# One PSUM bank of the attention scores changes its ring: two for the maxima, three for the exponentials

## The chip, the cores and the metric

The kernel runs on one core of a Trainium2 chip. The metric is the device time of one execution in microseconds. The kernel before takes 1253.35 us, the median of three runs (1252.35 to 1255.59).

## What is computed

Four sequences of 512 tokens with 512 channels go through two attention layers and a mixture of experts. Cut to what matters:

```python
# layer 1, x: (4, 512, 512), 16 heads of 32
xn = rms_norm(x, g_norm) * (1 + scale) + shift          # scale, shift from cond
q, k, v = split(xn @ W_qkv); q, k = rms_norm(q, g_q), rms_norm(k, g_k)
o = softmax(q @ k.T / sqrt(32)) @ v
y = o + o @ W_out
# layer 2: latent projections, rotary parts, causal attention
h = y + softmax(causal(q2 @ k2.T / sqrt(32))) @ v2 @ o_w
# 1 shared and 7 routed experts, the best two of them for each token
out = x + h + shared(rms_norm(h)) + sum(w_e * expert_e(rms_norm(h)))
```

Each softmax is over 512 keys, and its row maximum is subtracted before the exponential.

## The kernel before, in words

The attention of both layers is one loop over 512 steps. There are 8 batches (`k`): 0 to 3 are the four sequences in layer 1, 4 to 7 the same in layer 2, which is causal. A batch has 64 steps: 8 pairs of heads, in each pair 8 steps, which alternate between the two heads (`side`) and go through the four blocks of 128 tokens (`t`). `head_step` turns a step's number M into these.

For each step a block of scores is computed twice. `scores(M)` (matmul L939) writes scores with queries on the partitions, 128x512, and VectorE takes their row maximum (L1722 in layer 1; L1725 in layer 2, where a block is only (t+1)*128 wide and a second small instruction reads the accumulator). After each pair the maxima are transposed (`turn_max`, L948), ScalarE copies them (L1140, `max_rows`), and a DMA (L565) puts them as one more row under the pair's stacked operands (`stack`). `scores_t(M)` (L960, in layer 2 with a second small matmul for the mask, L963) then writes the transposed scores, keys on the partitions, with the maximum already subtracted by that row. ScalarE takes their exponential into `probs` (L1298), and `pv(M)` (L976; two rows of the trace for one product) multiplies them with the values. So each step's PSUM traffic goes through two rings of banks: `sq`, which is filled by L939 and cleared by the maximum, and `sk`, which is filled by L960 and cleared by the exponential.

The eight PSUM banks are dealt out by hand: 0 and 1 are the ring of all other work, `sq` has 2, 3 and 6, `sk` has 4 and 5, and 7 gathers the products with the values. A ring's item m lies in bank `banks[m % n]`, and `wait_free` before filling waits for the clearing of item m - n:

```python
def wait_free(self, eng, m):
    m = self.item(m)
    if m >= self.n:
        eng.wait_ge(self.free[m % self.n], m // self.n)
```

The order of every engine's work is written out. TensorE's loop does for step M: the scores of step M + 16 (`LEAD`), now and then `turn_max`, the transposed scores of step M, every fourth step the four products of steps M - 5 to M - 2 (`LAG`, `GROUP`), and then what the table `beside_heads` puts beside this step:

```python
for M in range(NSTEPS + LAG):
    if M + LEAD < NSTEPS:
        scores(M + LEAD)
    if M < NSTEPS:
        if max_turn(M) is not None:
            turn_max(max_turn(M))
        scores_t(M)
    if (M - LAG) % GROUP == GROUP - 1 and M > LAG:
        for n in range(GROUP):
            pv(M - LAG - GROUP + 1 + n)
```

Before the loop the scores of the first 16 steps are computed alone; this is called the lead below. Beside the steps go the projections (L793 to L795), transposes (L802), the output product and the splitting of fp32 values into a high and a low part. VectorE does the maximum of step M + 16 and then its own share of the table: scaling of transposed values out of PSUM (L1573, L1575), low halves (L1563), reciprocals and division, and the chains of norms (L1553 to L1559). ScalarE does the exponential of step M and then copies, squares and high halves. GpSimd makes low halves and squares in SBUF. A step of the table stands at the same step on each engine, with a step's delay for some. No scheduler reorders anything; each engine takes its list in program order.

After the loop the tiles of the experts use the same banks: transposed rows in 4 and 5 (`XB`), gate and up in 2 and 3 (`GB`), transposed hidden values in 6 (`HB`), the down product in 7. Their first uses wait for the last readers of those banks in the loop (`tile_turn`, `gate_up`, `turn_h`).

Of the kernel before, what the change touches and what calls it, by code (L numbers as in the profile page):

```python
# [42 lines left out]
NSTEPS = NB * STEPS_H  # L43
# [258 lines left out]
def build(nc, x_d, cond_d, wemb_d, bemb_d, gnorm_d, wqkv_d, gq_d, gk_d, wout_d, ln1_d, ln2_d, kvd_d,  # L302
# [11 lines left out]
    with ExitStack() as ctx:  # L314
        sem = lambda name: ctx.enter_context(nc.semaphore(name))
# [149 lines left out]
        r_ld, x1_ld, acc_ok, acc_st, x2_st = sem("second_x_loaded"), sem("residual_loaded"), sem("acc_ready"), sem("acc_stored"), sem("x2_rows_stored")  # L465
        lg_ok = sem("logits_ready")
        ring = Ring("ring", sem, (0, 1), RING_NO)
        sq = Ring("scores", sem, (2, 3, 6))
        sk = Ring("scoresT", sem, (4, 5))
        o = Ring("pv", sem, (7,))  # L470

        es_ld, es_hi, es_lo = (sem(f"shared_{x}") for x in ("loaded", "hi", "lo"))
# [313 lines left out]
        def _(pe):  # L786
# [226 lines left out]
            def tile_turn(i):  # L1013
                if i in ROUTED:
                    pe.wait_ge(xg_got[i % 2], 16 * (ROUTED.index(i) // 2 + 1))
                else:
                    pe.wait_ge(xg_ld[i % 2], 16 * (i // 2 + 1))
                if i >= 2:
                    pe.wait_ge(x_lo, i - 1)
                else:  # L1020
                    sk.wait_read(pe, NSTEPS - 2 + i)
                for c in range(NC):
                    last = nc.tensor.transpose(psum[:, XB[i % 2], c * P:(c + 1) * P], xg[:, i % 2, c * P:(c + 1) * P],  # L1023
                                               ident[:, :])
                last.then_inc(t_mm, 1)
# [34 lines left out]
            def turn_h(i):  # L1060
                q = i % 2
                pe.wait_ge(h_v, i + 1)
                if i >= 2:
                    pe.wait_ge(h_lo, i - 1)
                elif i == 0:
                    sq.wait_read(pe, NSTEPS - 3)
                for n in range(NI):
                    last = nc.tensor.transpose(psum[:, HB, (q * NI + n) * P:(q * NI + n + 1) * P],  # L1068
                                               hv[:, q, n * P:(n + 1) * P], ident[:, :])
                last.then_inc(h_mm, 1)  # L1070
# [23 lines left out]
            def table_product(n):  # L1094
# [5 lines left out]
                last.then_inc(g_mm_r, 1)  # L1100

            tile_turn(0)
            tile_turn(1)
            beside(("back", LAST, NPR - 1))
            gate_up(0, 0)
# [4 lines left out]
            for s in range(NTILES):  # L1110
                if s + 1 < NTILES:
                    gate_up(s + 1, 0)
                turn_h(s)
                if s + 2 < NTILES:
                    tile_turn(s + 2)
                if s == X2_SLOT:
                    beside(("x2", LAST, 0))
                    beside(("x2", LAST, 1))
                if s == ROUTER_SLOT:
                    beside(("router", LAST, 0))  # L1120
                for n in TABLE_MID.get(s, ()):
                    table_product(n)
                if s + 1 < NTILES:
                    gate_up(s + 1, 1)
                if s == COUNT_SLOT:
                    count_product()
                for n in TABLE_LATE.get(s, ()):
                    table_product(n)
                down(s)
                if s == X2_SLOT:  # L1130
                    beside(("x2", LAST, 2))
                    beside(("x2", LAST, 3))
                if s == ROUTER_SLOT:
                    beside(("router", LAST, 1))
# [897 lines left out]
```

## Time and profile before

| what | value |
|---|---|
| median of 3 runs | 1253.35 us (1252.35 to 1255.59) |
| profiled execution, own time | 1256.78 us |
| its span | 1255.0 us |
| TensorE busy in the span | 1145.3 us (91%) |
| VectorE / ScalarE / GpSimd busy | 728.1 / 572.9 / 333.9 us |
| mean granted clock of TensorE | 0.96 |
| lead, attention loop, rest | 77 to 89, 89 to 912, 912 to 1255 us |

The profile is of one execution. An engine's busy time counts its instructions, and for TensorE the matmuls; PEld are the weight loads that go ahead of them. In a row of a wait or a group, what stands behind the arrow ended the engine's idle time. The chain of work that ended last is 73% TensorE.

### The profile page before, as it was taken

Reading aid. Unit: us, or ns where it says so; the run is one execution under the profiler, and the core shown is the slowest. Engines: PE = TensorE matmul, PEld = TensorE weight load, DVE = VectorE, ACT = ScalarE, POOL = GpSimd, SP = SyncE. Lnnn points to the kernel's source line nnn. Section 1 sums busy time; section 2 is a strip of 40 time slices with the busy share of each in tenths; the row PEclk is TensorE's granted clock in tenths of the full one; section 3 lists DMA queues with packets and bytes.
Section 4 is the critical chain, followed back from the end, with each engine's and each line's share of the span. In section 5 each row is a group of like instructions: output and inputs, shape, how many; then the busy total and the mean of one; then the engine's idle time right before and its main releaser. Section 6 shows DMA issues by size and latency. Waiting matters only on the chain.

```text
span 1255.0 us, 18112 instructions
## 1 busy us (share of the span) xinstructions
PE 1145.3 (91%) x5687; PEld 798.4 (64%) x5687; DVE 728.1 (58%) x1714; ACT 572.9 (46%) x1248; POOL 333.9 (27%) x275
## 2 busy tenths in 40 slices
PE   5989989999999899999989899989989999999960
PEld 5755545665666456557657667755657888888850
DVE  6465486468545865656646766574545764444433
ACT  3324365445544565555455555544456743222310
POOL 0413133201320231002022202200235644555530
PEclk9969999999999899999989999998999999999985
DMA  7153344336322742553584473486567735656569
GB/s 262 34 168 118 98 145 130 90 98 202 120 64 89 228 131 64 184 168 105 175 229 140 144 247 95 144 250 162 145 215 249 250 126 106 109 111 116 106 147 328
DMA packets 105609, 191.10 MB, mean 152 GB/s; under 512 B 24140, under 2 KB 34796, under 8 KB 103980
## 3 DMA queue, kind: packets, MB, share of 16 engines
q1 hardware_dynamic: 96700, 169.61, 43.7%
q0 software_dynamic: 8512, 19.93, 8.9%
q8 instruction: 49, 0.80, 0.3%
q10 hardware_dynamic: 304, 0.40, 0.1%
q14 instruction: 44, 0.36, 0.1%
HBM read 118.98 MB, written 65.53 MB: 147 GB/s over the span
## 4 chain that ended last, share of the span: by engine, by line
PE 73%; DMA 8%; DVE 7%; SPq 4%; issue 3%; ACT 3%; POOL 1%; DVEq 0%; ACTq 0%; POOLq 0%
PE psum L976 12%; PE psum L793 9%; PE psum L794 8%; PE psum L795 8%; PE psum L939 6%; PE psum L960 6%; PE psum L1054 4%; PE psum L1056 4%; PE psum L1055 4%; PE psum L802 3%; PE psum L1081 2%; SPq L554 2%; PE psum L1083 2%; PE psum L1082 2%; PE psum L1023 2%
## 5 line engine op out<-in xcount | busy, mean ns | idle before, releaser
L1298 ACT ACTIVATE probs<-psum 128x512 f32<-128x512 f32 (+3 forms) x512 | 257.4, 517 | 217.2 <-PE psum L963 108.9
L1722 DVE TENSOR_REDUCE nmax<-psum 128x1 f32<-128x512 f32 x256 | 171.3, 686 | 124.2 <-PE psum L939 119.4
L939 PE MATMUL psum<-stack 96*128 96x512 f32 (+3 forms) x512 | 211.0, 417 | 10.1 <-DVE nmax L1725 6.7
L976 PE MATMUL psum<-probs,vals 128*33 128x512 f32 (+3 forms) x1024 | 212.3, 537 | 0.0
L960 PE MATMUL psum<-stack 97*128 97x512 f32 (+3 forms) x512 | 199.7, 391 | 11.8 <-ACT probs L1298 6.2
L1725 DVE CUSTOM_DVE_ANT_0 psum<-psum,causal 128x128 f32<-128x128 f32 (+3 forms) x256 | 123.8, 503 | 74.6 <-PE psum L939 73.6
L939 PEld LDWEIGHTS psum<-stack 96*128 96x128 f32 x512 | 100.5, 196 | 83.2 <-issue 58.4
L960 PEld LDWEIGHTS psum<-stack 97*128 97x128 f32 x512 | 99.7, 195 | 38.8 <-ACT probs L1298 16.7
L1433 POOL TENSOR_TENSOR o_lo<-o_chunk,o_hi 128x512 fp32r<-128x512 f32 x31 | 42.0, 1354 | 276.4 <-ACT o_hi L1140 276.4
L976 PEld LDWEIGHTS psum<-probs,vals 128*33 128x33 f32 x1024 | 50.0, 112 | 101.5 <-issue 76.4
L793 PE MATMUL psum<-w_hi,xh 128*128 128x512 f32 (+1 forms) x256 | 96.8, 378 | 5.2 <-POOL xl L1401 3.6
L794 PE MATMUL psum<-w_hi,xl 128*128 128x512 f32 (+1 forms) x256 | 94.9, 371 | 0.0
L795 PE MATMUL psum<-w_lo,xh 128*128 128x512 f32 (+1 forms) x256 | 94.6, 370 | 0.0
L1501 POOL DMA_INDIRECT acc_s<-tile_y,row_of_slot x38 | 60.5, 1591 | 82.4 <-DVE tile_y L1802 74.0
L1140 ACT ACTIVATE qk<-psum 128x512 f32<-128x512 f32 (+1 forms) x64 | 31.5, 493 | 101.6 <-PE psum L795 101.4
L1339 ACT ACTIVATE tile_h_hi<-psum 128x256 fp32r<-128x256 f32 x54 | 20.8, 385 | 99.2 <-PE psum L1068 98.8
L793 PEld LDWEIGHTS psum<-w_hi,xh 128*128 128x128 f32 x256 | 49.3, 193 | 22.6 <-issue 6.7
L1054 PE MATMUL psum<-routed_hi,tile_x_hi 128*128 x152 | 62.6, 412 | 0.0
L963 PE MATMUL psum<-mask,identr 128*128 128x128 f32 x256 | 61.4, 240 | 0.0
L1420 POOL TENSOR_TENSOR vs<-qk 128x512 f32<-128x512 f32 x32 | 33.6, 1051 | 103.3 <-ACT qk L1140 103.3
L1401 POOL TENSOR_TENSOR split<-vs,split 128x512 fp32r<-128x512 f32 x16 | 21.2, 1328 | 146.9 <-ACT split L1140 146.9
L1056 PE MATMUL psum<-routed_lo,tile_x_hi 128*128 x152 | 59.6, 392 | 0.0
(245 smaller groups left out, 2283.1 us busy)
## 6 DMA issues: line engine op xcount, KB each, us to landing
stack<-split_s SPq DMA_DIRECT2D x378, 128.0 KB, 3.3
split_s<-split SPq DMA_DIRECT2D x64, 512.0 KB, 3.9
inverse_sums<-inverse_s SPq DMA_DIRECT2D x31, 256.0 KB
xt<-in_x_dram SPq DMA_DIRECT2D x4, 1024.0 KB, 5.3
x_s<-yt SPq DMA_DIRECT2D x4, 1024.0 KB, 5.6
xt<-x_s SPq DMA_DIRECT2D x4, 1024.0 KB, 5.3
res<-x_s SPq DMA_DIRECT2D x4, 1024.0 KB, 10.3
yt<-in_x_dram SPq DMA_DIRECT2D x4, 1024.0 KB, 6.0
```

The lines of the kernel that those rows point to most:

```text
L793: nc.tensor.matmul(out, ah, bh, start=(i == 0), stop=False)
L794: nc.tensor.matmul(out, al, bh, start=False, stop=False)
L795: last = nc.tensor.matmul(out, ah, bl, start=False, stop=(i == n - 1))
L939: sq.filled(nc.tensor.matmul(psum[:, sq.bank(M), 0:n], st[:, 0, t * P:(t + 1) * P], st[:, 1, 0:n], start=True, stop=True), M)
L960: last = nc.tensor.matmul(psum[:, bank, lo:S], st[:, 1, t * P:(t + 1) * P], st[:, 0, lo:S], start=True, stop=not masked)
L963: last = nc.tensor.matmul(psum[:, bank, lo:lo + P], identr[:, :], mask[:, :], start=False, stop=True)
L976: nc.tensor.matmul(psum[at_:at_ + VW, o.bank(p), lo:S], vals[k % 2][:, t, head_of(q, side), :], probs[:, M % NX, lo:S], start=(t == 0), st ...
L1054: nc.tensor.matmul(out, xth[:, q, c, :], weight(i, 0, c), start=(c == 0), stop=False)
L1056: last = nc.tensor.matmul(out, xth[:, q, c, :], weight(i, 1, c), start=False, stop=(c == NC - 1))
L1298: sk.cleared(nc.scalar.activation(probs[:, M % NX, lo:S], psum[:, sk.bank(M), lo:S], ACT.Exp, scale=SCALE), M)
L1722: sq.cleared(V.tensor_reduce(out, psum[:, sq.bank(M), :], AX.X, ALU.max, negate=True), M)
L1725: sq.cleared(V.tensor_tensor_reduce(out=x, in0=x, in1=causal[:, (NT - 1 - t) * P:], scale=-1.0, scalar=-NEG, op0=ALU.add, op1=ALU.min, acc ...
```

## The change

The third bank of the scores for the maxima, bank 6, becomes the third bank of the transposed scores. The waits after the loop follow: `tile_turn` for tiles 0 and 1 waits for the exponentials of the last three steps, and `turn_h` for the last one, since bank 6 is now read by ScalarE. Instructions and their order are the same on every engine. Below the second hunk all line numbers grow by one.

```diff
-        sq = Ring("scores", sem, (2, 3, 6))
-        sk = Ring("scoresT", sem, (4, 5))
+        sq = Ring("scores", sem, (2, 3))
+        sk = Ring("scoresT", sem, (4, 5, 6))
...
                 if i >= 2:
                     pe.wait_ge(x_lo, i - 1)
                 else:
-                    sk.wait_read(pe, NSTEPS - 2 + i)
+                    for m in range(NSTEPS - 3, NSTEPS):
+                        sk.wait_read(pe, m)
...
                 elif i == 0:
-                    sq.wait_read(pe, NSTEPS - 3)
+                    sk.wait_read(pe, NSTEPS - 1)
```

## Rows read from the trace of the kernel before

**Rows 1.** The page, busy us of each engine (share of the span) xinstructions.
```profile
PE 1145.3 (91%) x5687; PEld 798.4 (64%) x5687; DVE 728.1 (58%) x1714; ACT 572.9 (46%) x1248; POOL 333.9 (27%) x275
```
**Rows 2.** Stretches: length, then PE, PEld, DVE, ACT, POOL busy; clock, DMA share, GB/s.
```profile
77.00:89.00 12.00, 10.72 (x20) 5.54 (x21) 10.55 (x18) 1.36 (x3) 2.93 (x5) 0.50 0.89 259
89.00:447.00 358.00, 344.16 (x1489) 207.08 (x1488) 226.82 (x404) 179.86 (x361) 84.15 (x68) 0.97 0.41 125
447.00:912.00 465.00, 436.69 (x2423) 296.70 (x2421) 281.39 (x878) 243.59 (x600) 73.02 (x72) 0.97 0.55 160
722.20:725.60 3.40, 3.40 (x12) 1.16 (x9) 1.77 (x6) 0.21 (x1) 0.00 (x0) 0.50 0.41 138
174.60:180.00 5.40, 5.40 (x23) 3.16 (x24) 4.03 (x6) 3.76 (x9) 3.78 (x3) 1.00 0.45 151
```
**Rows 3.** Waits of PEld, the weight loads: us in total, times, longest us.
```profile
PEld psum L960 <- ACT probs L1298: 16.7, 34, 1.8
...
PEld psum L939 <- DVE nmax L1725: 9.9, 13, 2.1
...
PEld psum L939 <- DVE nmax L1722: 4.4, 11, 1.5
```
**Rows 4.** Waits of PE, the matmuls: us in total, times, longest us.
```profile
PE psum L960 <- ACT probs L1298: 6.2, 17, 1.4
```
**Rows 5.** Groups by form: busy us, mean ns of one, then idle before, releasers.
```profile
L1298 ACT ACTIVATE probs<-psum 128x512 f32<-128x512 f32 x320 | 184.8, 596 | 127.5 <-PE psum L960 105.8 <-PE psum L963 21.0
L1722 DVE TENSOR_REDUCE nmax<-psum 128x1 f32<-128x512 f32 x256 | 171.3, 686 | 124.2 <-PE psum L939 119.4
```
**Rows 6.** Waits of DVE: us in total, times, longest us.
```profile
DVE nmax L1722 <- PE psum L939: 119.4, 76, 6.1
DVE psum L1725 <- PE psum L939: 73.6, 73, 3.7
```
**Rows 7.** Timeline at 174 us: start, us, engine, line, operation, [idle before].
```profile
173.41 0.64 ACT L1140 ACTIVATE wout_hi<-wout_raw 128x512 fp32r<-128x512 f32 x1
173.93 0.61 ACT L1298 ACTIVATE probs<-psum 128x512 f32<-128x512 f32 x1
...
174.59 0.19 PEld L960 LDWEIGHTS psum<-stack 97*128 97x128 f32 x1 [1.80 <-ACT probs L1298]
```
**Rows 8.** Timeline at 323 us, steps 143 to 145 of the scores.
```profile
323.03 0.80 DVE L1575 TENSOR_SCALAR vs<-psum,modall 128x512 f32<-128x512 f32 x1
...
323.32 0.19 PEld L939 LDWEIGHTS psum<-stack 96*128 96x128 f32 x1
...
323.98 0.69 DVE L1722 TENSOR_REDUCE nmax<-psum 128x1 f32<-128x512 f32 x1
...
324.11 1.91 PE L976 MATMUL psum<-probs,vals 128*33 128x512 f32 x8
...
325.53 0.69 DVE L1722 TENSOR_REDUCE nmax<-psum 128x1 f32<-128x512 f32 x1
```
**Rows 9.** Timeline of the lead and of the loop's first steps.
```profile
78.73 9.65 DVE L1722 TENSOR_REDUCE nmax<-psum 128x1 f32<-128x512 f32 x16
...
87.87 0.29 PEld L939 LDWEIGHTS psum<-stack 96*128 96x128 f32 x1 [0.94 <-DMA stack<-split_s]
...
88.70 0.69 DVE L1722 TENSOR_REDUCE nmax<-psum 128x1 f32<-128x512 f32 x1 [0.32 <-PE psum L939]
...
89.32 0.33 PEld L939 LDWEIGHTS psum<-stack 96*128 96x128 f32 x1
```
**Rows 10.** Timeline at 905 us, the last scores of the loop.
```profile
905.87 0.14 DVE L1725 DVE_READ_ACCUMULATOR2_ANT nmax<- 128x1 f32 x1
905.87 0.19 PEld L939 LDWEIGHTS psum<-stack 96*128 96x128 f32 x1
```
**Rows 11.** Timeline at 721 us, a wait for a maximum.
```profile
721.36 0.44 PE L939 MATMUL psum<-stack 96*128 96x384 f32 x1 [0.98 <-DVE nmax L1725]
```

## The prediction

> **What bounds the kernel now.** I start with the page's busy times [rows 1]: TensorE is busy 1145.3 of 1255.0 us, VectorE 728.1. The table by stretches [rows 2] splits that. The attention loop runs from 89 to 912 us; in its first half (batches in the order of the first layer) TensorE is busy 344.16 of 358.00 us, in the second (the causal layer) 436.69 of 465.00. So TensorE, which takes everything in program order, is the bound in both, and whatever makes it wait is paid in full unless it was about to wait anyway.
>
> The change touches two of its waits. Before writing scores of step M (L939) TensorE waits until VectorE's maximum has left that bank; before the transposed scores (L960) until ScalarE's exponential has. Today the first wait looks three steps back, the second two. The wait tables show what each costs: the weight loads of L960 wait 16.7 us for ScalarE in 34 places, those of L939 9.9 and 4.4 us for VectorE in 13 and 11 [rows 3]. The matmul rows, which hide a wait shorter than the matmul before it, show 6.2 us in 17 places for L960 [rows 4]. So the scarce side on record is the one that gets the bank. What the tables do not show is how much the third bank now saves on the other side; for that I go to the durations and the timeline.
>
> A maximum takes 686 ns and an exponential 596 ns on 512 columns [rows 5]. VectorE, though the idler engine, carries the bulky extras between maxima, and it waits for TensorE 119.4 and 73.6 us in 76 and 73 places [rows 6]: mostly it is early, and in bursts late.
>
> **The change, part by part.**
>
> *No instruction is added or moved.* Each engine keeps its rows; only which step's release a matmul waits for differs. At the tail `tile_turn` takes three waits where it had one, and `turn_h` waits for the last exponential instead of a maximum. The products with the values before them in TensorE's program already waited for those exponentials. Both cost nothing; that cover is gone only if the tail moved ahead of the last products.
>
> *Gain: the exponentials get three banks.* A typical place is 174.59 us [rows 7]: ScalarE has a weight copy before exponential 43, which ends at 173.93 + 0.61; TensorE's load for transposed scores 45 stands idle 1.80 us for it. With three banks it would need exponential 42, long done. The products behind do need 43, but only the last of the four does, and eight rows of products (two per product) take 1.91 us [rows 8], so three of them cover about 1.4 us. Going along all 512 transposed scores, I find about 50 loads that start within 75 ns of the end of the exponential two steps before, most at the steps in which the four products follow; their excess over the normal pitch of 0.235 us sums to 11.2 us. The tables bound it from below by 6.2 and from above by 16.7 us. I take 11.2 less 2.8 for those places in which VectorE's wait then stands in the same spot, **-8.4 us**.
>
> *Loss, in the lead.* From 78.73 us VectorE does 16 maxima in 9.65 us, 0.603 us each, and paces TensorE [rows 9]. At the clock of that stretch (0.50 of full, 1.2 GHz, [rows 2]) a load that was let go at 87.87 us is followed by its maximum at 88.70, 0.83 us later. With two banks two maxima need 0.69 + 0.05 + 0.83 = 1.57 us (0.05 is the shortest time seen from a release to a load), 0.785 each. So 14 x 0.18 = 2.6 us more. The load at 87.87 ends a wait of 0.94 us for a transfer that does not depend on this; it swallows as much. **+1.7 us**.
>
> *Loss, beside the lead.* With two banks a load of L939 must start 0.05 us after the maximum two steps before ends. The first place where it would not is early: maximum 16 ends at 88.70 + 0.69 = 89.39, load 18 stands at 89.32, 0.12 us short [rows 9]. The typical large one is at 323 us [rows 8]: VectorE alternates maxima with value scalings (0.80 us, L1575), 1.5 us a step, while TensorE puts two scores back to back ahead of four products. Load 145 starts at 323.32; maximum 143 runs from 323.98 to 324.67. Short by 1.40 us, and the 1.91 us of products behind it move as a block. Maximum 145 began at 325.53 because VectorE was late, not TensorE; hence it stays, and the shift ends in TensorE's time alone.
>
> I compare each of the 496 loads after the lead with that release: 112 are short, by 71 us together. That sum is wrong as a price, since a shift made by the first serves the next. In each stretch I carry the shift along: it becomes the larger of itself and the next shortfall, is reduced by any wait for VectorE that stands in the row today, and is booked when VectorE again waits for TensorE. The first stretch is that of 89.32 us, the last that of 905.87 us, where maximum 509 is read until 906.01 and the load is 0.19 short [rows 10]. There are 41 stretches with 25.2 us: by batches 6.4, 4.0, 2.9, 2.9 in the first layer, 1.5, 2.7, 1.2, 3.5 in the causal one, where today's waits of L939 [rows 3] already pay for much of it. **+25.2 us**.
>
> *A page's rule.* In the rows at 323 us rotation through banks alone does not overlap the read: maximum 143 starts 0.66 us after load 145 already stands. The Trainium skill, page "Perfetto Trace Analysis", section "Optimizing Tensor Performance", says that independent groups of matmuls should rotate through different banks so that one's evacuation overlaps the next group's work, and names no depth. Read so, two banks would do, and the loss beside the lead would be nought; the row speaks against it, and it comes back among the rivals.
>
> *Clock.* The loop runs at 0.97 of full clock on average, that is mostly at 2.4 GHz with a few stretches at 1.2. One of these lasts from 722.20 to 725.60 us [rows 2], right behind a wait for a maximum of 0.98 us [rows 11], and TensorE is busy through all of it. Half its 3.40 us, 1.7 us, is what such a stretch costs. New waits of over 1 us may bring one more or none: bounds 0 and 11 x 1.7 us, since 11 of my stretches are longer than 1 us. The idle 1.80 us at 174.59 brought none: behind it the clock is 1.00 [rows 2, 7]. So I take one, **+1.7 us**.
>
> Sum: -8.4 + 1.7 + 25.2 + 1.7 = **+20.2 us** on the profiled execution, whose own time is 1256.8 us for a span of 1255.0. That one lies 3.4 us above the median of the three runs, 1253.35. Against the median I forecast **1273.5 us**. A measurement of this kernel can tell about 0.3%, 3.8 us, from no change.
>
> **The rivals.**
>
> *Every wait cools the clock.* The clock falls behind most of the 11 long waits: 11 x 1.7 = 18.7 instead of 1.7 us, +37 us, **1290 us**. For: 722.20 lies right behind such waits. Against: the idle time at 174.59 us, which no fall follows. The Trainium skill, page "TensorE: Matmul & The Clock Gate", section "A second HAM failure mode: psum-queue depth-cycling", describes this for a kernel that cycles through banks, with small idle times between groups and a clock that swings. 15%.
>
> *VectorE's lateness spreads.* My carrying rule assumes that a late maximum holds only TensorE. If the extras behind it (scalings, low halves) come late too and TensorE waits for them, each stretch counts with its largest shortfall and nothing is swallowed: 39 + 1.7 + 1.7 - 8.4 = +34 us, **1287 us**. For: ScalarE and GpSimd follow VectorE's scalings. Against: today's waits of that kind are few. 12%.
>
> *Two banks are enough, and the third pays where it goes* (the other side, and the page's rule). TensorE is late itself when it reaches the scores: the lead of 16 steps keeps the loads behind, the first shift of a batch leaves VectorE a head start that lasts, and nothing but the lead's 1.7 us is lost, against a gain of 8.4 us or, by [rows 3], at most 16.7: -6.7 to -15.0 us, **1238 to 1247 us**. It decides if the load at 323 us comes 1.4 us later by itself. For: VectorE waits 193 us for TensorE in all [rows 6]. Against: a head start is lost whenever it waits, since its extras are tied to steps. 6%.
>
> *They cancel.* Losses half of mine, gain full: 12.6 + 1.7 - 11.2 = +3.1 us, **1256.5 us**. 6%.
>
> **How the numbers follow.** Forecast 61%, rivals 15, 12, 6 and 6%. The time is that of the forecast. The range reaches down to the forecast's terms at their kind ends (-16.7 + 1.7 + 25.2 + 0 = +10.2 us, 1263.5) less a little for stretches that I price too high, 1260, and up past both slower rivals, 1293. Out of it lie the last two rivals and some of the tail. Faster by over 0.3%: 0.06; within: 0.06; slower: 0.88.
>
> **What would show it.** Right: the loads of L939 wait for maxima some 30 to 45 us instead of 14.3, the loads of L960 for exponentials nearly nothing, with a few us turned up at the products' loads; the lead's 16 maxima take about 12 us instead of 9.65; at the place of 323 us a load stands idle some 1.4 us; the time after the loop is unchanged. Of the added time, two thirds lie in the first layer. Wrong: the attention loop is no longer than 823 us (my carrying rule fails), or L960 still waits for ScalarE (then the exponentials' lateness is more than one step deep), or the granted clock of the loop falls well below 0.97 (then the first rival).

## The result, and the profile after

The changed kernel takes 1268.82 us, the median of four runs (1263.02 to 1276.72), against 1254.47 us for the kernel before beside it: a ratio of 1.0113, 95% interval 1.0082 to 1.0145, so 14 us or 1.1% slower. Run again on another occasion (below), the ratio was 1.0121 (1.0094 to 1.0148). The forecast was 1273.5 us, 20 above the kernel before, in a range of 1260 to 1293.

The profiled execution of the changed kernel took 1266.78 us, its span is 1265.0. TensorE is busy 1149.0 us where it was 1145.3. Its weight loads wait, by the table of waits (us in total, times, longest us; of before see [rows 3]; lines above 1018 are one higher now):

```profile
PEld psum L939 <- DVE nmax L1723: 35.0, 48, 3.4
PEld psum L939 <- DVE nmax L1726: 20.3, 28, 2.7
...
PEld psum L976 <- ACT probs L1299: 3.7, 6, 0.7
```

The loads of the scores now wait 55.3 us for maxima where it was 14.3. The loads of the transposed scores no longer appear with ScalarE at all: the 16.7 us are gone. They did not turn up at the products' loads, as the forecast expected: those (L976) wait 3.7 us for exponentials, where it was 16.3. Where the time lies shows best when both traces are cut at the same four places: the first score, the first transposed score, the first transposed score of layer 2, and the last product with the values. First the kernel before, then the changed one, columns as in [rows 2]:

```profile
77.10:88.00 10.90, 9.71 (x18) 4.69 (x18) 9.88 (x17) 1.26 (x3) 2.93 (x5) 0.50 0.89 255
88.00:550.20 462.20, 444.95 (x1957) 265.93 (x1957) 290.85 (x549) 239.29 (x489) 99.30 (x83) 0.98 0.43 129
550.20:929.40 379.20, 353.03 (x2054) 248.19 (x2053) 225.19 (x754) 195.37 (x498) 66.62 (x62) 0.96 0.57 167
929.40:1255.00 325.60, 280.81 (x1422) 231.74 (x1422) 161.44 (x318) 112.97 (x218) 147.31 (x99) 0.94 0.65 167
```
```profile
75.60:89.30 13.70, 11.18 (x18) 4.67 (x19) 10.62 (x17) 1.23 (x3) 2.92 (x5) 0.50 0.83 243
89.30:557.90 468.60, 448.22 (x1957) 264.58 (x1958) 291.63 (x551) 239.81 (x489) 98.61 (x83) 0.98 0.42 126
557.90:939.50 381.60, 354.04 (x2054) 250.30 (x2052) 226.63 (x753) 195.49 (x497) 66.56 (x62) 0.96 0.57 165
939.50:1265.00 325.50, 281.03 (x1424) 231.85 (x1422) 161.64 (x319) 113.08 (x218) 147.28 (x99) 0.94 0.65 168
```

The lead is 2.8 us longer, layer 1 6.4, layer 2 2.4, the rest 0.1 shorter. The first score happened to start 1.5 us earlier, which makes the 10.0 us between the spans. The granted clock of each piece is the same to the two digits shown, but in layer 2 the changed kernel's trace has 34 us at half clock and that of before 27.

The typical place of [rows 8], the turn from batch 1 to batch 2, is there as forecast: load 145 has to wait for maximum 143. Timeline of the changed kernel, steps 143 to 145:

```profile
330.72 0.19 PEld L939 LDWEIGHTS psum<-stack 96*128 96x128 f32 x1 [0.23 <-issue]
...
331.47 0.69 DVE L1723 TENSOR_REDUCE nmax<-psum 128x1 f32<-128x512 f32 x1
...
332.22 0.19 PEld L939 LDWEIGHTS psum<-stack 96*128 96x128 f32 x1 [1.18 <-DVE nmax L1723]
...
332.89 1.91 PE L976 MATMUL psum<-probs,vals 128*33 128x512 f32 x8
```

Load 145 is the one at 332.22. It waits for maximum 143 to end at 332.16 and starts 0.06 us later; the products are behind it.

### The profile page after: what moved, and what is told of

Same layout as the page of the kernel before. It is cut to its first block, busy times and chain, and to the rows that moved or that the text cites. A ratio compares the mean times of both kernels' runs of the same rounds, so it can differ in the third digit from the quotient of the medians.

```text
span 1265.0 us, 18114 instructions
## 1 busy us (share of the span) xinstructions
PE 1149.0 (91%) x5687; PEld 797.1 (63%) x5687; DVE 731.3 (58%) x1714; ACT 573.7 (45%) x1248; POOL 333.1 (26%) x275
## 4 chain that ended last, share of the span: by engine, by line
PE 74%; DVE 9%; DMA 7%; SPq 3%; issue 3%; ACT 3%; POOL 0%; DVEq 0%; ACTq 0%; POOLq 0%
PE psum L976 13%; PE psum L793 9%; PE psum L795 8%; PE psum L794 8%; PE psum L939 8%; PE psum L960 6%; PE psum L1055 4%; PE psum L1057 4%; PE psum L1056 4%; PE psum L802 3%; PE psum L1082 2%; PE psum L1084 2%; PE psum L1083 2%; PE psum L1024 2%; DVE nmax L1723 2%
## 5 line engine op out<-in xcount | busy, mean ns | idle before, releaser
L939 PE MATMUL psum<-stack 96*128 96x512 f32 (+3 forms) x512 | 216.3, 426 | 32.1 <-DVE nmax L1726 15.3
L976 PE MATMUL psum<-probs,vals 128*33 128x512 f32 (+3 forms) x1024 | 214.5, 542 | 0.0
L960 PE MATMUL psum<-stack 97*128 97x512 f32 (+3 forms) x512 | 195.3, 382 | 3.3 <-DMA stack<-max_rows 3.2
L939 PEld LDWEIGHTS psum<-stack 96*128 96x128 f32 x512 | 100.2, 196 | 121.9 <-issue 57.7
L976 PEld LDWEIGHTS psum<-probs,vals 128*33 128x33 f32 x1024 | 50.4, 113 | 104.3 <-issue 92.0
L960 PEld LDWEIGHTS psum<-stack 97*128 97x128 f32 x512 | 100.2, 196 | 16.8 <-DMA stack<-max_rows 4.2
L793 PE MATMUL psum<-w_hi,xh 128*128 128x512 f32 (+1 forms) x256 | 95.6, 374 | 4.0 <-POOL xl L1402 2.3
L793 PEld LDWEIGHTS psum<-w_hi,xh 128*128 128x128 f32 x256 | 48.6, 190 | 21.3 <-issue 6.7
```

Source lines behind the costliest of these rows:

```text
L793: nc.tensor.matmul(out, ah, bh, start=(i == 0), stop=False)
L939: sq.filled(nc.tensor.matmul(psum[:, sq.bank(M), 0:n], st[:, 0, t * P:(t + 1) * P], st[:, 1, 0:n], start=True, stop=True), M)
L960: last = nc.tensor.matmul(psum[:, bank, lo:S], st[:, 1, t * P:(t + 1) * P], st[:, 0, lo:S], start=True, stop=not masked)
L976: nc.tensor.matmul(psum[at_:at_ + VW, o.bank(p), lo:S], vals[k % 2][:, t, head_of(q, side), :], probs[:, M % NX, lo:S], start=(t == 0), st ...
```

## The experiments

All ratios are to the kernel before, run in turn with them on the same chip. Four sets ran together: `two_two`, `layer2_exp`, `layer1_exp` and `lead_max`; `by_need` and `by_no_need`; `changed_again`, `two_two_again`, `need_idle` and `by_need_again`; and the last two.

### What is the exponentials' third bank worth?

`two_two` leaves bank 6 unused in the loop:

```diff
         sq = Ring("scores", sem, (2, 3))
-        sk = Ring("scoresT", sem, (4, 5, 6))
+        sk = Ring("scoresT", sem, (4, 5))
```

> Two banks for the maxima, two for the exponentials, bank 6 idle: the loss of the change without its gain. Theory (the third bank was worth 8 us to the exponentials, and that much of the loss was paid back): about 8 us above the changed kernel, 22 above the one before, and the loads of L939 wait for maxima about as long as in the changed kernel. Rival (once the loads of L939 wait for VectorE, ScalarE is never late, so the exponentials' third bank is worth nothing): equal to the changed kernel within 2 us, and the loads of L960 wait for exponentials under 4 us.

Measured: 1266.73 us, ratio 1.0091 (1.0069 to 1.0113). That is not above the changed kernel's 1.0113. My theory asked for about 1.018, so it falls, and the rival holds in its first half. In its second, under 4 us of waits for exponentials, it does not: the loads of L960 still waited 7.2 us. Since the two had not stood beside each other, I ran both once more:

> The changed kernel unaltered, to stand beside the next one on one chip. Both theories: 11 to 14 us above the kernel before.

> Bank 6 idle, on the same chip as the changed kernel. Theory as it stands now (ScalarE is late in the same stretches as VectorE, so a wait for a maximum covers what the exponentials' third bank would save): within 2 us of the changed kernel, at most 2 above. Rival (the third bank of the exponentials is worth the 8 us that I put on it): 8 above it.

Measured: 1268.13 us, 1.0121 (1.0094 to 1.0148), and 1268.25 us, 1.0122 (1.0097 to 1.0147). In the time as a whole the third bank of the exponentials is worth nothing that can be measured; by the two intervals up to some 4 us either way would not have shown. The waits of `two_two`'s loads:

```profile
PEld psum L939 <- DVE nmax L1723: 34.7, 48, 2.6
PEld psum L939 <- DVE nmax L1726: 18.2, 26, 3.0
PEld psum L976 <- ACT probs L1299: 16.2, 52, 0.4
PEld psum L960 <- ACT probs L1299: 7.2, 17, 0.8
```

Of the 16.7 us for exponentials before, more than half is gone though the exponentials got no bank: the likely reading is that TensorE, held back by the new waits for maxima, comes later to the exponentials' banks. What became of the other 7.2 can be seen where my forecast took its example [rows 7]. The changed kernel, loads of scores 61, 62 and 63, and what VectorE does meanwhile:

```profile
175.48 0.19 PEld L939 LDWEIGHTS psum<-stack 96*128 96x128 f32 x1 [1.07 <-DVE nmax L1723]
...
177.99 0.19 PEld L939 LDWEIGHTS psum<-stack 96*128 96x128 f32 x1 [0.84 <-issue]
...
178.47 1.19 DVE L1555 TENSOR_SCALAR rst<-sst 128x4 int32<-128x4 int32 x1
179.69 1.19 DVE L1556 TENSOR_SCALAR rst<-rst 128x4 int32<-128x4 int32 x1
180.91 0.69 DVE L1723 TENSOR_REDUCE nmax<-psum 128x1 f32<-128x512 f32 x1
...
181.66 0.19 PEld L939 LDWEIGHTS psum<-stack 96*128 96x128 f32 x1 [3.37 <-DVE nmax L1723]
```

and the second run of `two_two`:

```profile
176.54 0.19 PEld L939 LDWEIGHTS psum<-stack 96*128 96x128 f32 x1 [0.92 <-DVE nmax L1723]
...
177.54 0.19 PEld L960 LDWEIGHTS psum<-stack 97*128 97x128 f32 x1 [0.81 <-ACT probs L1299]
...
179.81 0.19 PEld L939 LDWEIGHTS psum<-stack 96*128 96x128 f32 x1 [0.84 <-issue]
...
182.73 0.19 PEld L939 LDWEIGHTS psum<-stack 96*128 96x128 f32 x1 [2.63 <-DVE nmax L1723]
```

With two banks the load of transposed scores 45 waits 0.81 us for an exponential; with three it does not, and load 62 comes 2.51 instead of 3.27 us after load 61. Then load 63 waits 3.37 instead of 2.63 us, and from load 61 to load 63 it is 6.18 us in the one and 6.19 in the other. TensorE reaches the next wait for VectorE earlier and waits there.

How much is left in sum can be read from the waits of all matmuls added up, whatever they wait for: 68.7 us before, 76.6 and 75.7 in the two profiles of `two_two`, 74.7 in both of the changed kernel. So the exponentials' third bank saves 1 to 2 us of TensorE's waits, not 8.

That leaves the clock, and there the two kernels differ. The mean granted clock is 0.963 in the 74 executions of the kernel before that ran beside the experiments, 0.957 in the 10 of the changed kernel and 0.961 in the 11 of `two_two`. What is missing to a full clock, (1 - clock) times the span, is 45.9, 54.8 and 49.5 us on average, with standard errors of 0.4, 1.3 and 1.3. So a small gain of the third bank may be eaten by a lower clock. Single profiles do not settle it. Layers 1 and 2 in `changed_again` and then in `two_two`:

```profile
89.90:559.30 469.40, 448.27 (x1957) 265.11 (x1957) 291.12 (x549) 239.91 (x489) 98.41 (x83) 0.98 0.41 126
559.30:937.20 377.90, 350.88 (x2054) 248.24 (x2053) 225.99 (x754) 195.84 (x498) 66.44 (x62) 0.96 0.57 167
```
```profile
90.10:560.20 470.10, 449.58 (x1958) 265.58 (x1958) 291.10 (x551) 240.00 (x489) 98.36 (x83) 0.98 0.42 125
560.20:943.20 383.00, 353.74 (x2054) 248.91 (x2053) 226.91 (x754) 196.34 (x498) 66.79 (x63) 0.96 0.57 166
```

In layer 2, at a clock of 0.96 in both, `changed_again` is 5.1 us shorter; but the two other profiles of the same kernels have it the other way round, 381.60 us at 0.96 and 378.50 at 0.98. Why the clock is lower with three banks for the exponentials stays open.

### Where does the loss sit: which layer, and the lead?

For these, bank 6 changes hands during the loop. Each of banks 2 to 6 gets one pair of semaphores, a table is dealt out in TensorE's program order, and a matmul takes the bank of its set that was used longest ago. Instructions and their order stay. The matmuls after the loop wait for the last readers of both sets. Only the rule that says for which scores m bank 6 belongs to the maxima differs; it stands for RULE in this cut.

```diff
-        sq = Ring("scores", sem, (2, 3))
-        sk = Ring("scoresT", sem, (4, 5, 6))
+        full, free = ({b: sem(f"scores_{x}{b}") for b in (2, 3, 4, 5, 6)} for x in ("full", "free"))
+        of = deal(RULE)
+        sq, sk = Dealt(of["sq"], full, free), Dealt(of["sk"], full, free)
...
+    for M in range(-LEAD, NSTEPS):
+        S_ = M + LEAD
+        mine = third_to_maxima(S_)
+        if S_ < NSTEPS:
+            take("sq", (2, 3, 6) if mine else (2, 3))
+        if M >= 0:
+            take("sk", (4, 5) if mine else (4, 5, 6))
```

`layer2_exp`, with the rule `m < 16 + 4 * STEPS_H`:

> Bank 6 goes to the maxima in the lead and in layer 1, to the exponentials in layer 2. Theory (loss where VectorE alternates bulky work with full-width maxima, which is layer 1): 0 to 4 us above the kernel before, and layer 1 as long as before. Rival (the loss belongs to the ring, in whatever layer): half of the measured 14 us, so 7 above.

Measured: 1255.4 us, 1.0004 (0.9987 to 1.0021). Level with the kernel before, as the theory had it; the rival's 7 us are outside. In its profile layer 1 takes 460.10 us (462.20 before). In layer 2 the loads of scores wait 18.7 us for maxima, 8.8 more than before, and those of the transposed scores 8.4 us less for exponentials, and the time is level.

`layer1_exp`, with `m >= 16 + 4 * STEPS_H`:

> The mirror image: bank 6 goes to the exponentials in the lead and in layer 1, to the maxima in layer 2. Theory: 9 to 12 us above the kernel before. Rival (loss even over the layers): 7 above.

Measured: 1265.74 us, 1.0096 (1.0065 to 1.0127), 12 us by the ratio and 10 between the medians: the lead and layer 1 carry the loss. Its profile has a lead of 13.70 us and 470.60 us for layer 1:

```profile
76.20:89.90 13.70, 11.17 (x18) 4.66 (x18) 10.59 (x17) 1.25 (x3) 2.93 (x5) 0.50 0.84 243
89.90:560.50 470.60, 449.66 (x1957) 265.39 (x1957) 291.05 (x549) 240.14 (x489) 98.47 (x83) 0.98 0.42 125
```

`lead_max`, with `m < LEAD`:

> The changed kernel, but the 16 scores of the lead take three banks in turn. Theory (each two maxima of the lead need 1.57 instead of 1.21 us): the lead is 2.5 to 3 us shorter than in the changed kernel and the rest the same, so 2 to 3 us below it. Rival (the transfer of the stack ends last anyway): no shorter than the changed kernel.

Measured: 1265.29 us, 1.0090 (1.0063 to 1.0117). The runs don't tell it from `two_two` beside it. The profile does: the lead is back at 10.90 us, with 16 maxima in one go again, and layer 1 stays as long as in the changed kernel.

```profile
75.60:86.50 10.90, 9.77 (x18) 4.76 (x19) 9.89 (x17) 1.24 (x3) 2.94 (x5) 0.50 0.84 254
86.50:555.20 468.70, 447.57 (x1957) 264.63 (x1957) 291.17 (x551) 240.01 (x489) 98.73 (x83) 0.98 0.42 127
```

So the lead costs 2.8 us; that the whole program is shorter by as much is consistent with the runs and not shown by them.

### Is it the places where VectorE is late?

The 20 stretches are those in which a load of L939 in the trace of before stands less than 0.05 us behind the end of the maximum two steps back, with the two scores ahead of it, and with stretches merged that have at most three scores between them; they begin with scores 0 to 33 and end with 458 to 511. They hold 256 of the 512 scores, so that the mirror image shares bank 6 exactly as evenly.

> Bank 6 belongs to the maxima for 256 of the 512 scores, in 20 stretches: those in which the trace of the kernel before shows a maximum two steps back that is late for a load of L939 (the lead among them). In the other 256 it belongs to the exponentials. Theory (the loss of the change sits where VectorE is late, nowhere else): as fast as the kernel before, within 2 us, or up to 3 us faster if the exponentials gain in the other half. Rival (the maxima need their third bank anywhere, in proportion to the steps): 6 us above the kernel before.

Measured: 1251.36 us, 0.9985 (0.9972 to 0.9998).

> The mirror image: bank 6 belongs to the exponentials in those 20 stretches and to the maxima in the other 256 scores. Theory: as slow as the changed kernel, 11 to 14 us above the kernel before, with the loads of L939 waiting for maxima over 45 us. Rival (in proportion to the steps): 6 us above.

Measured: 1267.45 us, 1.0116 (1.0093 to 1.0140). With bank 6 the same half of the time in maxima's hands, one is level with the kernel before or a hair faster and the other as slow as the changed one. The rival, 6 us for each, is out. So the place decides; part of the difference may come by way of the clock, whose mean is 0.965 in `by_need` and 0.958 in `by_no_need`. The waits of `by_need` and then of `by_no_need` (their lines are shifted: L991 is the scores, L1012 the transposed ones, L1028 the products):

```profile
PEld psum L1012 <- ACT probs L1352: 15.3, 32, 1.8
PEld psum L991 <- DVE nmax L1779: 10.7, 13, 2.0
...
PEld psum L991 <- DVE nmax L1776: 6.1, 13, 1.5
```
```profile
PEld psum L991 <- DVE nmax L1776: 34.2, 46, 3.4
PEld psum L991 <- DVE nmax L1779: 18.0, 28, 2.4
...
PEld psum L1028 <- ACT probs L1352: 11.0, 29, 0.7
...
PEld psum L1012 <- ACT probs L1352: 1.2, 3, 0.7
```

This also tells why the other term failed. In `by_need` the exponentials have three banks in half of the loop, and yet 15.3 of 16.7 us of waits for them are left: they lie inside the stretches in which VectorE is late. Given the bank inside those stretches, in `by_no_need`, they vanish, and waits for maxima stand there instead. To see what the exponentials' bank earns outside the stretches, `need_idle` leaves bank 6 idle there. Its expectation speaks of 16.6 of 18.2 us of waits; the rows for the loads of transposed scores say 15.3 of 16.7:

> As by_need, but outside its 20 stretches bank 6 is idle instead of the exponentials'. Theory: equal to by_need within 1 us, since 16.6 of the 18.2 us of waits for exponentials were still there in by_need, that is, they lie inside the stretches. Rival (by_need's small gain comes from the exponentials): 2 us above it, level with the kernel before.

> by_need unaltered, beside need_idle on one chip: 1 to 3 us below the kernel before if its small gain is real, level with it if that was chance.

Measured: `need_idle` 1250.53 us, 0.9993 (0.9976 to 1.0009), `by_need` again 1251.19 us, 0.9980 (0.9964 to 0.9996). The two medians are 0.7 us apart and the intervals overlap. `by_need` is 0.15 to 0.2% below the kernel before in both of its sets, just clear of equal; whether that comes from the exponentials stays open. Its mean clock, 0.965 in both sets, lies above the 0.963 and 0.964 of the kernel before beside it, which may be part of it or all.

### What makes VectorE late at the worst place?

The wait of 3.37 us above stands behind operations on 128x4 numbers that take 1.19 us each, while GpSimd splits weights. Both were there in the kernel before, only without a matmul waiting. `changed_norm_later` moves the norm parts of batch 0 four steps on in the changed kernel, `by_need_norm_later` does so in `by_need`:

```diff
-            put((44, 45, 46, 47), norm)
+            put((48, 49, 50, 51) if k == 0 else (44, 45, 46, 47), norm)
```

> The changed kernel with the four norm parts that VectorE does beside batch 0 four steps later, so that they no longer meet GpSimd's two weight splits. There three operations on 128x4 numbers take 0.74, 1.19 and 1.19 us instead of 0.17 and hold the maximum behind them; the load of score 63 waits 3.37 us. Theory (the price of the missing bank is set by how late VectorE is at a few places, and here it is GpSimd that makes it late): that wait falls below 1 us and batch 0 of the loop is 1.5 to 3 us shorter than the changed kernel's 124 us. Rival (VectorE's work is the same, so another place pays): batch 0 as long as before.

> The same four parts moved in by_need, in which that stretch has three banks for the maxima and shows no wait for VectorE there. Theory (three banks already hide this lateness): equal to by_need within 1 us, 1 to 3 us below the kernel before. Rival (GpSimd's hold on VectorE costs TensorE time in any case): 1.5 to 3 us below by_need.

Measured: 1268.8 us, 1.0106 (1.0072 to 1.0139), and 1253.01 us, 0.9984 (0.9965 to 1.0003). In the first the load of score 63 no longer waits and the two operations are back at their usual length (groups of its profile: busy us, mean ns):

```profile
L1555 DVE TENSOR_SCALAR rst<-sst 128x4 int32<-128x4 int32 x12 | 2.0, 170 | 0.4
L1556 DVE TENSOR_SCALAR rst<-rst 128x4 int32<-128x4 int32 x12 | 2.0, 170 | 0.4
```

Batch 0, from the first transposed score to the 65th, takes 122.7 us instead of 123.9 in the changed kernel: 1.2 us, less than the 1.5 to 3 that I expected, so much of the wait came back elsewhere. The runs show neither gain, and the second kernel is equal to `by_need`, as expected.

## Why the prediction was right, point by point

- **What bounds the kernel.** Right. TensorE's order, with VectorE late in bursts: the split by need shows it.
- **A row misread.** In the timeline at 323 us the prediction calls the maximum that starts at 325.53 number 145. It is number 144; 145 starts at 326.74. The argument, that VectorE is later there than the moved TensorE, holds all the more.
- **No instruction moved, the tail free.** Right: 325.60 and 325.50 us after the loop.
- **Gain of the exponentials, -8.4 us.** Wrong; in the time it measured 0, with `two_two` and the changed kernel at 1.0122 and 1.0121, and in TensorE's waits 1 to 2 us. The step that failed is the one that left 11.2 us but for 2.8 to be earned. The waits for exponentials were counted rightly, and they did disappear. But I had checked only that the products behind them give cover, and not where these waits lie: inside VectorE's late stretches, all but 1.2 to 1.4 us. There, at the place shown, the next wait for a maximum takes in what was saved.
- **Loss in the lead, +1.7 us.** Mis-sized: 2.8 us. The cycle was right (two maxima started at 78.77 and the next two at 80.35 in the changed kernel, 1.58 us; I had 1.57). Two things were missed. With two banks the load of score 16 waits for maximum 14, with three only for maximum 13, which is one maximum (0.6 us) more. And the transfer swallows less than 0.94 us: counted from the first load of scores, maximum 13 ended after 10.13 us and the transfer let go the load after 10.81, so 0.68. In the changed kernel maximum 14 ends after 13.47 us and the load of score 16 stands at 13.59. Its matmul ends a wait for a maximum, no longer one for the transfer:

```profile
89.14 0.77 PE L939 MATMUL psum<-stack 96*128 96x512 f32 x1 [0.28 <-DVE nmax L1723]
```

- **Loss beside the lead, +25.2 us.** The mechanism was right and the size more than twice too large. `two_two` bears the whole loss and no gain: 11 to 15 us by its two sets, of which 2.8 are the lead's, so 9 to 12, and up to 3.6 of these are the clock's (49.5 against 45.9 us above). In its matmul rows the waits for maxima rise by 22.3 us (7.5 before), but all waits together by only 7 to 8. The rest came off other waits: 3.4 us off those for exponentials (6.2 to 2.8), 2.7 off that of the transposes for VectorE's L1619, 3.0 off those of the projections (L793) for GpSimd, and smaller ones off transfers. My rule let only waits for VectorE swallow a shift, and had entered those for exponentials as a gain of its own. One and the same wait can be taken off once, and waits for other engines and for transfers shrank too. The sign to look for was missed as well: the loads of L939 wait 55.3 us for maxima and not 30 to 45, and yet the loss is smaller, since the sum of these waits is no price.
- **Clock, +1.7 us.** Too small. By the executions on record 8.9 us more than before are missing to a full clock (54.8 against 45.9). Among the 74 executions of the kernel before, 1 us of this goes with 0.5 us of time. So I estimate 4.5 to 9 of the 14 us, the upper end being what it costs when TensorE is busy throughout. The profiles alone hide this, since the one of before ran at 0.960 and the changed kernel's at 0.958. One new stretch at half clock does lie right behind a new long wait, the one of 3.37 us, where the kernel before had 1.00:

```profile
182.80:186.20 3.40, 3.40 (x10) 2.63 (x9) 2.68 (x9) 0.24 (x1) 0.00 (x0) 0.50 0.67 175
```

A stretch of the kernel before, 114.60 to 118.00 us at 0.50, is missing in exchange. With the 6.0 us by which the waits of all matmuls rise, the estimate makes 10 to 15 us, and 14 were measured. The first rival asked for 18.7 us by the clock and +37 in all; both are out.
- **The rivals.** "VectorE's lateness spreads", +34 us, is out by the size. "Two banks are enough" is out, since the kernel is slower: at the place named a load does wait 1.18 us. The rule of the Trainium skill, page "Perfetto Trace Analysis", section "Optimizing Tensor Performance", that independent groups should rotate through the banks, holds as far as it goes, but the number of banks in the rotation decided here. "They cancel" named a loss of half of mine, and that was nearer the truth than mine; the gain that was to cancel it was missing.
- **The split.** Two thirds in layer 1, as forecast, or more: 6.4 of 8.8 us in the loop's two layers, all of it in `changed_again` (469.40 and 377.90 us, against 462.20 and 379.20 before), and 10 to 12 of 14 us with the lead by `layer1_exp`.

The total came near by luck: a gain of 8 that was not there and a clock term that was 3 to 7 too small stood against a loss that was 13 to 16 too large.

## What to carry to other kernels

An engine that works in order can wait at one place for what it did not wait for at another. So before a wait is booked as a gain, look where it lies: if it shares its stretch with another engine's lateness, taking it away can merely move it to the next wait. Here the third bank belonged where the reader alternates with bulky work, though the tables of waits named the other reader: the bank that does its work shows no wait. To test such a thing, deal the bank by place and run the mirror image too. And compare the granted clock over all executions, not over one profile of each kernel.

## What the runs showed of the hardware

VectorE operations on 128x4 numbers take 0.17 us at the median and 1.20 at most in the kernel before (L1554). The long ones lie beside GpSimd's splits of 1.27 us each, as here in the timeline of before:

```profile
176.50 2.54 POOL L1446 TENSOR_TENSOR wout_lo<-wout_raw,wout_hi 128x512 fp32r<-128x512 f32 x2
176.61 1.20 DVE L1554 TENSOR_SCALAR rst<-sst 128x4 int32<-128x4 int32 x1
...
177.84 1.22 DVE L1555 TENSOR_SCALAR rst<-rst 128x4 int32<-128x4 int32 x1
```

Each of VectorE's lasts nearly as long as one of GpSimd's (1.20 and 1.22 us; the two of GpSimd take 2.54). Moved away from them by `changed_norm_later`, all twelve take 0.17 us. Why they take longer side by side is shown by no run.
